# One layer of attention with experts on one Trainium2 core: from step 17 on, a step's products with V and with ones stand together in the next step, expert rows are added earlier, and c is turned last and in full width

## The reference

```python
q, k, v = (proj(Wq), proj(Wk), proj(Wv))            # 16 heads of 32
q, k = _apply_rope(q, k)
scores = jnp.einsum('bhqd,bhkd->bhqk', q, k) / sqrt(32)
scores = jnp.where(causal, scores, finfo.min)
attn = softmax(scores)
out = jnp.einsum('bhqk,bhkd->bhqd', attn, v) -> (tokens, 512) @ Wo.T
...
top_vals, top_idx = jax.lax.top_k(xf @ gate_w.T, 2)  # 8 experts
out = sum over the 2 experts of w * (xf @ expert_w[e].T + expert_b[e])
```

## Time and profile before

| what | value |
|---|---|
| median of 3 runs | 984.97 us (984.73 to 988.17) |
| the profiled execution, its own time | 987.53 us |
| its span, first to last instruction | 985.8 us |
| mean granted TensorE clock | 0.987 of full speed |
| PE busy / DVE busy | 917.9 us (93%) / 744.3 us (76%) |
| POOL busy / ACT busy | 561.3 us (57%) / 436.6 us (44%) |

### The profile page before, as it was taken

One profiled execution on the slowest core, in us unless ns is written; L12 is line 12 of the kernel. 1 busy time (PEld: TensorE's weight loads), 2 busy tenths in 40 slices (PEclk: granted clock), 3 DMA queues, 4 the chain that ended last, 5 costly groups with the idle time before them and its releaser, 6 DMA issues.

```text
span 985.8 us, 18723 instructions
## 1 busy us (share of the span) xinstructions
PE 917.9 (93%) x6557; PEld 452.1 (46%) x6589; DVE 744.3 (76%) x1327; ACT 436.6 (44%) x711; POOL 561.3 (57%) x553
## 2 busy tenths in 40 slices
PE   2898898999999989989999999989999999999887
PEld 1344344444444544545555555544444444444333
DVE  7988988898789899944444444487788888888865
ACT  5367867766765433431122111124334444344432
POOL 1545676674776446763333333157878888778731
PEclk9999999999999999999999999999999999999999
DMA  6365589688786353485655555464655554565531
GB/s 243 109 223 198 179 269 320 199 306 293 211 275 260 119 204 97 187 291 192 198 176 178 172 171 174 148 214 141 193 177 188 172 194 141 163 189 159 173 103 55
DMA packets 107963, 188.63 MB, mean 191 GB/s; under 512 B 11872, under 2 KB 65248, under 8 KB 102624
## 3 DMA queue, kind: packets, MB, share of 16 engines
q1 hardware_dynamic: 97072, 152.03, 44.4%
q0 software_dynamic: 10800, 35.40, 12.5%
HBM read 117.13 MB, written 70.25 MB: 190 GB/s over the span
## 4 chain that ended last, share of the span: by engine, by line
PE 66%; DVE 14%; DMA 6%; ACT 5%; POOL 4%; issue 3%; SPq 1%; another core or an unknown queue 0%; DVEq 0%; ACTq 0%; POOLq 0%
PE psum L949 19%; PE psum L1034 10%; PE psum L1058 7%; PE psum L997 5%; PE psum L984 5%; PE psum L966 5%; PE psum L1000 5%; PE psum L1043 4%; PE psum L926 4%; DVE top L1483 3%; ACT pT L762 2%; DMA sum_sb<-x 2%; POOL k_hl L590 1%; PE psum L968 1%; DMA w_rows<-w_hl 1%
## 5 line engine op out<-in xcount | busy, mean ns | idle before, releaser
L762 ACT ACTIVATE pT<-psum,factors 128x512 f32<-128x512 f32 (+1 forms) x352 | 218.2, 642 | 244.0 <-PE psum L984 226.8
L1483 DVE TENSOR_REDUCE top<-psum 128x1 f32<-128x384 f32 (+3 forms) x352 | 210.4, 634 | 22.0 <-PE psum L968 16.6
L1034 PE MATMUL psum<-xT,w_att 128*128 128x512 f16 x768 | 195.7, 380 | 6.7 <-DVE xT L1434 4.7
L949 PE MATMUL psum<-w_exp,x_gT 128*128 x852 | 195.3, 379 | 0.6 <-DVE x_gT L1439 0.6
L610 POOL DMA_INDIRECT x_g<-xn_rows,tok_of x71 | 67.5, 951 | 131.5 <-PE psum L926 129.6
L966 PE MATMUL psum<-k_stack,q_stack 96*128 96x384 f16 (+3 forms) x512 | 127.8, 303 | 15.6 <-DVE top L1483 13.0
L984 PE MATMUL psum<-q_stack,k_stack 98*128 98x256 f16 (+3 forms) x512 | 129.5, 306 | 11.0 <-ACT pT L762 8.9
L1439 DVE TENSOR_TENSOR x_gT<-psum,x_gT 128x512 f16<-128x512 f32 x71 | 49.0, 692 | 104.1 <-ACT x_gT L786 90.7
L949 PEld LDWEIGHTS psum<-w_exp,x_gT 128*128 128x128 f16 x852 | 83.4, 98 | 85.5 <-issue 0.9
L786 ACT ACTIVATE x_gT<-psum 128x512 f16<-128x512 f32 x71 | 42.3, 597 | 170.0 <-PE psum L926 170.0
L600 POOL TENSOR_TENSOR o_hl<-o_sb,o_hl 128x512 f16<-128x512 f32 x31 | 36.5, 1178 | 127.9 <-ACT o_hl L776 123.2
(11 more groups left out here) (175 smaller groups left out, 1301.9 us busy)
## 6 DMA issues: line engine op xcount, KB each, us to landing
y_rows<-y_sb SPq DMA_DIRECT2D x71, 256.0 KB
w_in<-w_all SPq DMA_DIRECT2D x12, 1024.0 KB, 12.1
q_stack<-qk_rows SPq DMA_DIRECT2D x96, 128.0 KB
k_stack<-qk_rows SPq DMA_DIRECT2D x96, 128.0 KB
x_in<-x SPq DMA_DIRECT2D x8, 1024.0 KB, 10.2
qk_rows<-q_hl SPq DMA_DIRECT2D x32, 256.0 KB
qk_rows<-k_hl SPq DMA_DIRECT2D x32, 256.0 KB
xn_rows<-x_in SPq DMA_DIRECT2D x8, 1024.0 KB, 5.0
```

Of the source, the lines that this page charges most:

```text
L762: act.activation(p_of(j, h, heads), banks[BANK_T + (NT_ * n + k) % 2][:, 0:W], ACT.Exp, scale=factors[:, 0:1]).then_inc(exp_done, 1)
L949: now = pe.matmul(banks[s % 4], x_gT[s % 4][:, xp * C + c, :], w_exp[:, bass.ds(e, 1), wp, c, :].rearrange("p e d -> p (e d)"), start=n == ...
L1034: now = pe.matmul(bank, w_att[:, what, wp, c, g * P:(g + 1) * P], xT[b % 2][:, xp * C + c, :], start=at_pass == 0, stop=at_pass == 3 * C - 1)
L1483: return dve.tensor_reduce(out=top[:, h:h + heads, i], in_=banks[BANK_S + k % 2][:, 0:heads * W].rearrange("p (h t) -> p h t", h=heads), a ...
```

## The change

From step 17 on, `times_v` of all four key tiles of group n - 1 stands in step n, behind scores 3. In steps 16 to 30, `turn_c` moves behind the last shifted scores on PE, and `copy_c` moves on ACT behind `exps(n, 9)`. In all steps, `turn_c` transposes a 128-column tile whose columns 32 to 127 are zero (set once), instead of 32 columns; the copy still reads 32 rows. On DVE, `add_experts` moves from the end of the step to behind `largest_score(n + 1, 3)`, ahead of `normalise_o(n - 1)`.

```diff
--- before.py
+++ after.py
@@ -124,7 +124,8 @@
     top = at("top", [P, HG, J], F32)
     c_scale = at("c_scale", [P, HG * J], F32)
     c_f = at("c_f", [P, HG * J], F32)
-    c_hl = at("c_hl", [P, 2, HG * J], F16)
+    c_wide = at("c_wide", [P, P], F16)
+    c_hl = c_wide[:, 0:2 * HG * J].rearrange("p (f r) -> p f r", f=2)
     c_turn = at("c_turn", [2 * HG * J, P], F16)
     rden_few = at("rden_few", [P, S // HD], F32)
     w_att = at("w_att", [P, NQ, 2, C, D], F16)
@@ -815,7 +816,7 @@
                 if n + G < N:
                     take_v(n + G, BANK_QV)
                 exps(n, 8)
-                if n + 1 < N:
+                if n < N1:
                     copy_c(n + 1)
                 if n + 3 < N:
                     high_qk(1, n + 3)
@@ -823,6 +824,8 @@
                     high_x(TURN_AT[n], 0)
                     high_x(TURN_AT[n], 1)
                 exps(n, 9)
+                if N1 <= n < N - 1:
+                    copy_c(n + 1)
                 exps(n, 10)
                 if n in TURN_AT:
                     high_x(TURN_AT[n], 2)
@@ -970,7 +973,7 @@
 
             def turn_c(m):
                 pe.wait_ge(c_made, m + 1)
-                pe.transpose(half(BANK_S + 1)[0:2 * HG * J, 0:P], c_hl[:].rearrange("p f r -> p (f r)"), ident16[:]).then_inc(c_turned, 1)
+                pe.transpose(half(BANK_S + 1)[:, 0:P], c_wide[:], ident16[:]).then_inc(c_turned, 1)
 
             def shifted_scores(n, k):
                 h0, heads, j = T_UNITS[k]
@@ -1093,8 +1096,8 @@
                     free_bank_out(n)
                     spread_max(JOB_AT[n - 1])
                 if n and n != N1:
-                    times_v(n - 1, 2)
-                    times_v(n - 1, 3)
+                    for j in range(0 if n > N1 else 2, J):
+                        times_v(n - 1, j)
                 if n in KEEP_AT:
                     free_bank_out(n)
                     if n - 1 in JOB_AT:
@@ -1186,15 +1189,17 @@
                     if n == G:
                         pe.wait_ge(w_lo_done, 4)
                     project_out(wo[0], BANK_KO, 0, 4)
-                if nxt:
+                if n < N1:
                     turn_c(n + 1)
                 shifted_scores(n, 9)
                 if wo:
                     project_out(wo[0], BANK_KO, 4, 8)
                 shifted_scores(n, 10)
-                if nxt:
+                if n < N1:
                     times_v(n, 0)
                     times_v(n, 1)
+                elif nxt:
+                    turn_c(n + 1)
                 else:
                     times_v_last(0, 1, 2)
                 if wo:
@@ -1558,6 +1563,8 @@
                 if nxt:
                     largest_score(n + 1, 2)
                     largest_score(n + 1, 3)
+                for w in late_tiles(n):
+                    add_experts(w)
                 if n - 1 in JOB_AT:
                     scale_of(JOB_AT[n - 1])
                 if n == 1:
@@ -1621,9 +1628,8 @@
                     spread_low(1, 0)
                     spread_low(1, 1)
                     experts_of_tiles()
-                for w in late_tiles(n):
-                    add_experts(w)
-
+
+            dve.memset(c_wide[:], 0.0)
             own.link(dve.memset(c_scale[:], 2.0 ** -LOG_C))
             for u in range(2):
                 dve.memset(k_stack[u][ROW_C:ROW_C + 2, :, :], -2.0 ** LOG_C).then_inc(ones_made, 1)
```

## The result

Run beside each other, the changed kernel takes 998.56 us (median of 4 runs, 992.98 to 1000.69) and the kernel before 986.57 us (4 runs, 984.73 to 990.37): a ratio of 1.0099, 95% interval 1.0058 to 1.0141. It is slower by 1%: the medians lie 12.0 us apart, the ratio stands for 9.8 us, and both the time and the direction are outside what was predicted. The profiled execution of the changed kernel took 992.98 us, the fastest of its four, against 987.53 for the profiled one before. The profiles therefore show only about 5.5 us of the difference.

A forecast was written before the change was run, and what follows sets the result against it. PE was taken to bound the steps behind the experts, then a loop through POOL and ACT. Terms -2.0 + 4.1 - 1.3 + 0.2 - 1.2 = -0.2 us, from 984.97, gave 984.8 us; range 979.5 to 993.5.

The forecast's parts named there:

- ahead of the experts only the width of the turn changes: 16 steps ahead of the experts: the wider turn of c saves 0.1 to 0.2 us each, taken as -2.0 us.
- Step 16, +4.1 us: First step behind the experts: additions wait for gathered rows, delaying DVE's fifth maximum and PE; +4.1 us, from 2.5 to 8.
- some 5 us and then a little more: Step 16: how long DVE was expected to stand waiting for gathered expert rows.
- the 8.6 predicted: Step 16: DVE goes on to its fifth maximum at 659.4 us in the trace, 8.6 us late.
- the landing of the gathers: Step 16: the last of four gathers lands 3.6 us after issue, 4.2 at most; two additions follow.
- where 4.5 was predicted: Step 16: PE's work at its old wait for an exponential starts at 666.2 us, 4.5 us late.
- the 8 of its rival: Rival that step 16 costs its high end, 8 us instead of 4.1: 988.7 us in all; chance 8%.
- The loop, 20.7 us a step: Steps 17 to 27: a new loop through POOL and ACT's copy of c sets about 20.7 us, above PE's 20.37.
- The gain of eleven steps: Steps 17 to 27: each gains 0.1 us instead of PE's 0.44, together -1.3 us, ends -4.8 and +3.5.
- DVE and c: Behind the experts: additions fit before normalising (rival late DVE, +8.4 us, 13%); c's travel stays hidden (rival late c, 7%).
- The last steps, +0.2 and -1.2 us: Step 28 to 29 gets 0.2 us longer by the loop; the last three steps save 0.4 us each, -1.2.
- -2.3 was forecast for the steps behind step 16: Steps behind step 16: the terms -1.3 (eleven steps), +0.2 (28 to 29) and -1.2 us (last three) together.

The follow-up runs named there:

- changed_pad64: The changed kernel with 64 more unused bytes, so later tiles shift by 256 bytes instead of 192; 1.0046 of the kernel before, 993.35 us.
- before_pad: The kernel before with 192 unused bytes behind the tile of c, moving all later tiles, nothing else; 1.0037 of the kernel before, 992.80 us.
- changed_late16: The changed kernel, but in step 16 alone the expert rows are added at the step's end as before; 1.0031 of the kernel before, 991.14 us.
- before_pad256: The kernel before with 256 unused bytes behind the tile of c, moving all later tiles by 256 bytes; 0.9993 of the kernel before, 988.84 us.
- mixed_best: changed_late16 with turns wide only behind the experts and the wide tile behind the last slot, so no other tile moves; 0.9973 of the kernel before, 985.47 us.
- mixed_copy_first: mixed_best with ACT's copy of c ahead of the split of k, as in the kernel before; 0.9949 of the kernel before, 984.19 us.
- changed_again: The changed kernel run once more, unaltered, in 6 runs beside other variants; 1.0094 of the kernel before, 997.44 us.
- before_wide: The kernel before with the wide tile and wide turn of c alone, later tiles moved by 192 bytes; 1.0033 of the kernel before, 990.95 us.
- before_wide_behind: The kernel before with turns wide only behind the experts, wide tile behind the last slot, nothing else moved; 0.9960 of the kernel before, 984.89 us.

## Why the prediction was wrong, step by step

**The step that failed: "ahead of the experts only the width of the turn changes", -2.0 us.** The wide tile's price was looked for in its matmul and its memset, and not in its 192 bytes. They cost 4.7 us in the changed kernel (changed_pad64, 1.0046 for 1.0094), 3.7 thousandths or 3.7 us by themselves (before_pad, 1.0037). The -2.0 itself was too large as well: in the steps ahead of the experts that the shift leaves alone, a turn of c follows the last one as before or up to 0.2 us sooner (25.04 us for 25.25 and 24.72 for 24.86 in the last two), some 0.5 us in all, so little of it was on the path. No rival held this, and it is the largest single term that the sum lacked. The time would not have lain well inside the range without it: 998.56 - 4.7 is 993.9, against an upper bound of 993.5.

**Step 16, +4.1 us: right in mechanism, wrong in its terms.** The wait, its releaser and its place came as told, but it was longer. DVE stood 8.12 us where "some 5 us and then a little more" was expected, and did its fifth maximum 14.78 us behind scores 0 of the step (665.62 against 650.84) instead of 4.56 (650.81 against 646.25): 10.2 us late for the 8.6 predicted. PE stood 9.55 for 8, and POOL 5.42 us for DVE ahead of its rotation of q. The step that failed here is the landing of the gathers, taken as 3.6 us from the earlier trace rows, whose window begins behind the four gathers that count. These four took

```profile
DMA to landing us min/median/max: 4.9/5.5/6.4
```

and the slowest is the second, of the first tile (issued at 656.17), so that all four additions stand behind the wait and not two.

The total came out near the forecast by luck. PE reached the place of its old wait, the shifted scores of 384 columns, 7.4 us later than before (673.74 - 650.84 = 22.90 us behind scores 0, against 661.73 - 646.25 = 15.48), where 4.5 was predicted. But the work behind that place, which was slow before, now ran at the full clock. The lower clock lay over the wait and 3.6 us of work in the changed kernel, and over 6.0 us of work in the kernel before (first line after, second before; the clock is the third number from the end):

```profile
666.20:669.80 3.60, 3.57 (x11) 1.50 (x12) 2.80 (x6) 0.69 (x1) 1.78 (x2) 0.55 0.00 0
661.70:667.70 6.00, 5.97 (x18) 2.30 (x19) 4.84 (x3) 3.57 (x7) 5.65 (x6) 0.52 0.14 46
```

The same work up to the next scores 0 took 4.13 us (673.74 to 677.87) instead of 7.13 (661.73 to 672.01, less the 3.15 us of products that stood there), which gives 3.0 us back. In the profiles the stretch from the last expert matmul to the first normalising is 34.5 us (650.7 to 685.2) for 30.3, 4.2 us longer. In the medians step 16 costs 6.3 us (changed_late16), with an interval that holds the 4.1 of the sum and the 8 of its rival. Counted from scores 0, the four profiled kernels with this wait take 34.2 to 35.1 us, and the kernel before, before_pad, before_pad256, changed_late16 and mixed_best 29.0 to 30.1. The Trainium skill (TensorE: Matmul & The Clock Gate, What's actually happening) has the default throttled and activity releasing it. The trace after agrees with the page in that PE came out of its 9.55 us wait at the lower clock (0.50 us for 384 columns), and shows one such stretch and not a second.

**The loop, 20.7 us a step: right.** 20.65 measured, 0.28 us ahead of scores 0, the addition for k at 1.27 us; mixed_copy_first cuts the loop and finds PE's 20.37. The gain of eleven steps is (20.82 - 20.68) x 11 = 1.5 us for -1.3.

**DVE and c: right.** The additions fit with 0.43 us to spare. SP's wait for the store of c is 12.7 us in 10 steps, 2.3 at most, and PE waits for no load of c from 690 to 900, so its travel stays hidden. From issue to landing the store takes 1.4 us in the median, less than the 2.0 that the prediction took from the Trainium skill (DMA: Bandwidth & Descriptors, Anatomy of one DMA). The section tells that figure of DMAs that GpSimd issues; here SP issues them:

```profile
SPq L417 <- DMA c_rows<-c_turn: 12.7, 10, 2.3
```

**The last steps, +0.2 and -1.2 us: the +0.2 has the wrong sign, the sum is not told apart.** In the profiled execution the step from the turn at 904.13 to that at 925.72 takes 21.59 us, against 915.92 - 895.47 = 20.45 before. But it ran at a clock of 0.92. In changed_again, the same kernel, it ran at 1.00 and took 19.88 us:

```profile
904.13:925.72 21.59, 19.89 (x147) 9.25 (x146) 16.56 (x29) 9.34 (x17) 15.77 (x20) 0.92 0.52 159
903.87:923.75 19.88, 18.21 (x146) 8.74 (x145) 16.54 (x29) 8.12 (x15) 14.32 (x17) 1.00 0.57 173
```

So at equal clock this step is 0.6 us shorter and not 0.2 us longer. It and the two behind it together are 54.41 us (changed_again 55.51), against 56.57 in the kernel before and 55.56 in before_pad256, whose order is that of the kernel before: whether they gained more than the 0.6 us that they were given can't be told from the clock.

**The sum again.** The experiments that take out one part give shift +4.7 (changed_pad64), step 16 +6.3 (changed_late16) and everything else together -2.7 us (mixed_best, where -2.3 was forecast for the steps behind step 16): +8.3 us, against 9.3 (1.0094) and 9.8 us (1.0099) measured. Each of the three is uncertain by 2 to 4 us, so that they add up this well is partly chance. Of the 13.8 us between the forecast of 984.8 and 998.56, another 1.6 us are the starting point: the kernel before had a median of 986.57 us beside the changed one, and the forecast started from 984.97.

**What stays open.** Through which wait the shift costs its time. The profiles, one of each kernel, say where it lies. From the first turn of c to that of group 16, the eight kernels without a shift take 371.8 to 374.7 us (373.0 in the mean) and the six with 192 bytes under all tiles 372.9 to 378.9 (375.3). From there to scores 0 of step 16, the experts, it is 221.8 to 223.8 (222.5) and 222.7 to 226.2 (223.9). Most of what differs ahead of the experts lies in the steps between the sixth and the eleventh turn, and not in the same ones in each kernel. PE's wait for c ahead of the experts grew from the earlier trace rows 10.5 to

```profile
PE psum L976 <- DVE c_wide L1498: 12.6, 8, 3.1
```

in the changed kernel, but before_pad (10.6) and before_pad256 (10.7) show almost the same list of waits. Time times clock is 980.3 us in before_pad and 978.2 in the kernel before (uncertain by 1.3 and 0.9 us), while their mean times are 3.5 us apart; so by that figure, roughly, half of the cost is PE standing or working longer and half is clock. That slower transfers make PE stand a little longer at a few places, and that this costs clock, is argued, not shown.

Also open is what the wide turn does ahead of the experts by itself. No run has it there in the kernel before with unmoved tiles. before_wide (1.0033) is no faster than before_pad (1.0037), though its turns behind the experts are wide and these alone gave before_wide_behind 4.0 thousandths. By these three ratios the wide turns ahead of the experts cost 3.6 thousandths, uncertain by 3.9, where a gain of 2.0 us was forecast; the turns in the trace show no such cost.

## What to carry to other kernels

When a tile changes its size, look at what is placed behind it, and keep the offsets of tiles that DMAs write or read at the multiples of 256 bytes that they had (in this kernel leaving them cost 0.2 to 0.4%); a control kernel with unused bytes tells layout from logic. Before you move work ahead of a wait on an engine, look at the first pass through the loop, where the data is not there yet, and leave it out there; and take the time of a transfer from rows of that very place. An edit that shortens the bounding engine closes the next loop: read which copy stands behind which split, and put the one first that the bounding engine waits for.

## What the runs showed of the hardware that was not expected

- 192 unused bytes make the same transfers take 46.2 instead of 44.4% of the DMA engines' time (before_pad) and the kernel 1.0037 as long; 128 bytes 1.0024; 256 bytes 0.9993.
- changed_again and the kernel before differ in the mean granted clock by 0.9827 to 0.9905, which is 7.8 us of 1,000, while time times clock differs by 0.8 us. It does not hold of every pair: mixed_copy_first had a lower clock than the kernel before (0.9869 against 0.9889) and was faster.
- A longer wait can shorten the slow work behind it. After 3.73 us of waiting PE worked 6.0 us at a mean clock of 0.52, after 9.55 us 3.6 us at 0.55.
- The first four gathers of expert rows behind the experts land in 4.9 to 6.4 us (median 5.5), those issued from 660 us on in 3.3 to 6.9 us (median 3.9), in the same profile.
